# Queries and keys stored as rows 2d + s, in a LayerNorm + attention + mixture-of-experts kernel

## The chip, the cores and the metric

The kernel runs on one core of a Trainium2 chip. The metric is the device time of one execution in microseconds, as the median over several runs. Engines are called PE (TensorE), DVE (VectorE), ACT (ScalarE), POOL (GpSimd) and SP (SyncE, here only a queue that issues DMAs).

## What is computed

The input x has shape [2, 1024, 256]. It is normalized, and the output is x plus attention plus a mixture of experts, both of the normalized rows:

```python
xn = _layernorm(x, axis=-1)
x = x + attention(xn, W_q, W_k, W_v, W_o) + experts(xn, Wr, Wg, Wu, Wd)
```

Attention has 16 query heads of 16 dimensions and 4 heads of keys and values, each serving 4 query heads. Queries and keys are turned by rotary position angles, then softmax(q k / 4) v, then W_o. The experts: 8 of them, each token takes its top 2 by router logits, with a softmax gate over the two; an expert is silu(x Wg), clipped, times x Wu, times Wd. All of it is float32.

## The kernel before, in words

**Stages.** There are 2048 tokens, in 16 tiles of 128. First come LayerNorm, transposes, values and router logits, routing, and the projection of queries and keys (`queries_keys`). Then an expert loop over SLOTS = 39 slots, t = 0 to 38; a slot is one tile of 128 gathered token rows of one expert. Then attention over 8 head groups g (batch times key head), each in two halves h of 512 queries, so 16 halves.

**A slot of the expert loop.** POOL gathers the rows of slot t from xn_d in DRAM with an indirect DMA (`gather_rows`, L541, four row buffers go round; it waits until the transposes of slot t - 4 are done). PE does the gate and up product of slot t (`gate_up`, L1210), the transposes of slot t - 1's activations (L1218) and of slot t + 1's rows (L1203), and the down product of slot t - 2 (L1227). ACT does SiLU (L699) and copies the transposes (L702, L706), and stores finished rows to rows_out; DVE clips (L985), multiplies (L987) and copies the result (L993).

**Rope parts beside it.** The projected queries and keys are turned in 12 parts, at slots PART_SLOTS = 1, 3, 5, 7, 9, 11, 14, 17, 20, 23, 26, 29 (L307). In the order of PARTS (L302) parts 0, 1, 6 and 7 are keys (64 rows of 512 columns, made into 128 rows by two differences of column blocks), the others queries (128 rows of 512 columns). For part q, POOL or DVE multiplies by cos and sin (`times_cos`, `times_sin`, `rope_step`), DVE adds (L880, and L887, L889 for keys), ACT rounds to a high part (`high_part`, L683), DVE subtracts to get the low part (L899), and SP stores both to DRAM (`store_part`, L380). Buffers rope_a, rope_b, rope_hi and rope_low come four times (NB = 4), so `high_part(q)` waits until the stores of part q - 4 have landed (L682, through `stored_before`), and so does L899 (L898). ACT runs `high_part(5)` behind its work of slot 9.

**Rows.** A head's 16 dimensions are stored twice, as s = 0 (high) and s = 1 (low): q_hl has 32 rows for a head. Before, row s * 16 + d. The score product contracts 64 rows, in which high and low queries meet high (j = 0) and low (j = 1) keys.

**SP's queue** is in one order: all stores and loads that follow wait for what stands ahead of them. In the loop over the slots (L439) it stores part q at its slot; at t = 13 it waits for parts 0 and 1 to land (`parts_stored(1)`) and loads the key stack of group 0 (`load_ka`, 8 DMAs of 64 KB); at t = 14 it stores part 6 (keys), waits for parts up to 3 (`parts_stored(3)`) and loads the first queries (`load_q(0, 0, 0)`, L402, 4 DMAs of 128 KB); at t = 17 it stores part 7; at t = 18 it loads the second queries. Later slots load the second key stack (`load_kb`) and those of group 1 (LATE_LOADS).

**Scores beside the last slots.** From slot 18 = SLOTS - SHARED on, PE does the first scores of attention beside the slots (`first_max`, L1182, and `score_first`, L1149). The first of them, ahead of slot 18's gate product, waits for the first queries (`pe.wait_ge(q_loaded[v], 64)`, L1186).

**Attention.** ACT's exponentials (L740), PE's scores (L1280, L1284), products with values (L1294) and the score bounds of the half after next (L1155 to L1172), DVE's maxima (L934 to L942). In `period` SP loads kb of the next group, ka of the one after it and queries, a group ahead.

**Shapes of the accesses before.** A query store writes `[8, 16, 512]` from 128 partitions; a key store writes `[2, 64, 512]` from 128 partitions; a query load reads `[32, 2, 512]`; a load of ka or kb reads `[2, 16, 512]` (or fewer columns), its first dimension being a repetition of the same 16 rows, into 32 partitions.

Of the kernel before, what the change touches and what calls it, by code (L numbers as in the profile page):

```python
# [8 lines left out]
F32 = mybir.dt.float32  # L9
# [9 lines left out]
HD = 16  # L19
# [16 lines left out]
def build(nc, x, w_q, w_k, w_v, w_o, w_r, w_g, w_u, w_d, cos_t, sin_t, out):  # L36
# [3 lines left out]
    KV = w_k.shape[1] // HD  # L40
# [5 lines left out]
    HALF = S // 2  # L46
# [5 lines left out]
    NB = 4  # L52
# [14 lines left out]
    q_hl = nc.dram_tensor("q_hl", [B, NH, 2 * HD, S], F32, kind="Internal").ap()  # L67
    k_hl = nc.dram_tensor("k_hl", [B, 2, 2, KV * HD, 2 * HALF], F32, kind="Internal").ap()
# [3 lines left out]
    with ExitStack() as ctx:  # L72
        def sb(name, shape, dt=F32):
            return ctx.enter_context(nc.sbuf_tensor(name, shape, dt))
# [25 lines left out]
        rope_hi = [sb(f"rope_hi{m}", [P, HALF], F32R) for m in range(NB)]  # L100
        rope_low = sb("rope_low", [P, NB, HALF], F32R)
        rope_lo = [rope_low[:, m, :] for m in range(NB)]
# [199 lines left out]
        PARTS = [(k, m) for b in range(B) for k, m in ((2 * b, 2), (2 * b + 1, 2), (2 * b, 0), (2 * b, 1), (2 * b + 1, 0), (2 * b + 1, 1))]  # L302
# [19 lines left out]

        def stored_before(q):

            return 32 * len(range(q % NB, q, NB))


        def part_at(t):

            return PART_SLOTS.index(t) if t in PART_SLOTS else None  # L330
# [33 lines left out]
        def _(sp):  # L364
# [15 lines left out]
            def store_part(q):  # L380
                k, m = PARTS[q]
                n, done = q % NB, qk_stored[q % NB]
                b, cols = k // 2, slice(k % 2 * HALF, (k % 2 + 1) * HALF)
                sp.wait_ge(lo_ready, q + 1)
                if m < 2:
                    q_rows = q_hl[b, 8 * m:8 * m + 8, :, cols].rearrange("n (s d) q -> s n d q", s=2)
                    sp.dma_start(q_rows[0], rope_hi[n][:, 0:HALF].bitcast(F32)).then_inc(done, 16)
                    sp.dma_start(q_rows[1], rope_lo[n][:, 0:HALF].bitcast(F32)).then_inc(done, 16)
                else:
                    k_rows = [k_hl[b, k % 2, j].rearrange("d (u c) -> u d c", u=2) for j in range(2)]  # L390
                    sp.dma_start(k_rows[0], rope_hi[n][:, :].bitcast(F32)).then_inc(done, 16)
                    sp.dma_start(k_rows[1], rope_lo[n].bitcast(F32)).then_inc(done, 16)


            def load_q(g, h, i, heads=(0, 1)):
# [9 lines left out]
            def twice(g, j, half, cols):  # L405

                kv = g % KV
                return k_hl[g // KV, half, j, HD * kv:HD * (kv + 1), cols].unsqueeze(0).to_broadcast(
                    [2, HD, cols.stop - cols.start])

            def load_ka(g, p):

                for half in range(2):
                    for j in range(2):
                        low, high = 2 * HD * j, STACK + 2 * HD * j
                        sp.dma_start(ka[p][low:low + 2 * HD, half, :].bitcast(F32),
                                     twice(g, j, half, slice(QUART, KCOLS))).then_inc(ka_loaded[p], 16)
                        sp.dma_start(ka[p][high:high + 2 * HD, half, :].bitcast(F32),
                                     twice(g, j, half, slice(0, HALF))).then_inc(ka_loaded[p], 16)

            def load_kb(g, p):
                for half in range(2):
                    for j in range(4):
                        sp.dma_start(kb[p][2 * HD * j:2 * HD * (j + 1), half, :].bitcast(F32),
                                     twice(g, j % 2, half, slice(HALF - P, 2 * HALF - P))).then_inc(kb_loaded[p], 16)
# [9 lines left out]
            def parts_stored(last):  # L435
                for q in range(max(0, last - NB + 1), last + 1):
                    sp.wait_ge(qk_stored[q % NB], stored_before(q + NB))

            for t in range(SLOTS):  # L439
                q = part_at(t)  # L440
                if q is not None:
                    store_part(q)
                if t == KEYS_LOAD:
                    parts_stored(1)
                    load_ka(0, 0)
                if t == FIRST_LOAD:
                    parts_stored(3)
                    load_q(0, 0, 0)
                if t == SECOND_LOAD:
                    parts_stored(5)  # L450
                    load_q(0, 1, 1)
                for n in LATE_LOADS.get(t, ()):
                    sp.wait_ge(rows_t_ready, t)
                    if n == 0:
                        load_kb(0, 0)
                    elif n == 1:
                        load_ka(1, 1)
                    else:
                        load_q(1, (n - 2) // 2, 2 + (n - 2) // 2, [n % 2])
                if t == SLOTS - 7:  # L460
                    sp.wait_ge(m_turned_ready, 1)
                    load_m(0)
# [170 lines left out]
        def _(act):  # L633
# [44 lines left out]
            def high_part(q):  # L678
                n = q % NB
                act.wait_ge(rope_done, q + 1)  # L680
                if q >= NB:
                    act.wait_ge(qk_stored[n], stored_before(q))  # L682
                act.activation(rope_hi[n][:, :], rope_a[n][:, :], ACT.Copy).then_inc(hi_ready, 1)  # L683
# [67 lines left out]
        def _(dve):  # L751
# [140 lines left out]
            def rope_step(q):  # L892
                if 2 <= q <= NP + 1:
                    n = (q - 2) % NB
                    dve.wait_ge(hi_ready, q - 1)
                    dve.wait_ge(rope_done, q - 1)
                    if q >= NB + 2:
                        dve.wait_ge(qk_stored[n], stored_before(q - 2))  # L898
                    nc.vector.tensor_tensor(rope_lo[n], rope_a[n][:, :],  # L899
                                            rope_hi[n][:, :].bitcast(F32), ALU.subtract).then_inc(lo_ready, 1)  # L900
                if q < NP:
                    (k, m), n, rows_q = PARTS[q], q % NB, part_rows(q)
                    dve.wait_ge(pj_copied, 3 * k + m + 1)
                    if q >= NB:
                        dve.wait_ge(rope_done, q - NB + 1)
                    nc.vector.stream_shuffle(rope_b[n][0:rows_q, :], projected(k, m)[0:rows_q, :],
                                             [d ^ 1 for d in range(32)]).then_inc(swapped, 1)
                    if vector_cos(q):
                        if q >= NB:
                            dve.wait_ge(hi_ready, q - NB + 1)  # L910
                            dve.wait_ge(lo_ready, q - NB + 1)
                        nc.vector.tensor_tensor(rope_a[n][0:rows_q, 0:HALF], projected(k, m)[0:rows_q, :],
                                                cos_s[0:rows_q, k % 2 * HALF:(k % 2 + 1) * HALF], ALU.mult).then_inc(cos_done, 1)
# [507 lines left out]
```

## Time and profile before

| | us |
|---|---|
| median of 3 runs | 556.92 (556.55 to 557.96) |
| profiled execution, its time | 555.41 |
| its span | 553.6 |
| PE busy | 519.5 (94%) |
| DVE busy | 384.6 (69%) |
| ACT busy | 384.2 (69%) |
| POOL busy | 170.0 (31%) |
| mean granted clock of PE | 0.984 |

DMA moves 52.72 MB in 39266 packets, a mean of 95 GB/s. The chain of work that ended last is 79% PE, 8% DVE and 7% DMA, with 4% of the span under the stores of rope_low to k_hl and 2% under the loads of qs from q_hl.

The trace gives starts and durations in microseconds from the start of the span. Idle time stands in brackets with what released the engine. An issue on SP is timed as long as SP is held by it, which is not the time that the transfer takes; from issue to landing is given apart. A DMA share of 1/16 = 0.0625 is one of the 16 DMA engines busy. The granted clock is 1.00 at 2.4 GHz and 0.50 at 1.2 GHz.

### The profile page before, as it was taken

What the parts mean: (1) busy time and instruction counts of PE and PEld (TensorE: products, weight loads), DVE (VectorE), ACT (ScalarE), POOL (GpSimd) and SP (SyncE); (2) the same over time, 40 slices, a digit from 0 to 9 for tenths busy, and PEclk for the clock granted to TensorE, in tenths of its full rate; (3) what the DMA queues carried; (4) which work ended last, traced back from release to release, by engine and by line L of the source; (5) the groups of instructions that cost most, each with busy time, mean ns of one, the idle gap of its engine ahead of it and who ended that gap; (6) DMA issues with size and microseconds to landing.
All of it is one profiled execution on the core that took longest, in us unless ns stands there. A gap on an engine that the chain in (4) does not pass through costs nothing.

```text
span 553.6 us, 10341 instructions
## 1 busy us (share of the span) xinstructions
PE 519.5 (94%) x3626; PEld 247.9 (45%) x3626; DVE 384.6 (69%) x907; ACT 384.2 (69%) x551; POOL 170.0 (31%) x214
## 2 busy tenths in 40 slices
PE   8999987909999998999999999999999999999997
PEld 7833644504555554344444444444434444444433
DVE  4684886514787665778788788788787788885123
ACT  3534533302444335999999999999999999998673
POOL 4016654512232200032337332453245242510000
PEclk9999999958999999999999999999999999999999
DMA  8971455423345511131132131231132132200101
GB/s 292 374 219 38 113 153 161 147 93 113 119 140 164 153 38 40 41 95 41 60 96 67 53 96 49 68 96 52 55 92 76 48 92 59 58 3 22 49 28 58
DMA packets 39266, 52.72 MB, mean 95 GB/s; under 512 B 7632, under 2 KB 25424, under 8 KB 39216
## 3 DMA queue, kind: packets, MB, share of 16 engines
q1 hardware_dynamic: 26992, 34.35, 19.9%
q0 software_dynamic: 3408, 9.31, 6.0%
q10 hardware_dynamic: 8816, 8.40, 4.9%
q8 instruction: 30, 0.49, 0.4%
q14 instruction: 20, 0.16, 0.1%
HBM read 36.18 MB, written 15.60 MB: 94 GB/s over the span
## 4 chain that ended last, share of the span: by engine, by line
PE 79%; DVE 8%; DMA 7%; issue 3%; SPq 2%; ACT 1%; DVEq 0%; ACTq 0%
PE bank L1294 23%; PE bank L1284 10%; PE bank L1210 9%; PE bank L1155 9%; PE bank L1172 8%; PE bank L1227 4%; DMA k_hl<-rope_low 4%; PE bank L1124 4%; PE bank L1330 3%; PE bank L1280 3%; PE bank L1165 2%; DVE xn_t L942 2%; DVE xn L1019 2%; DMA qs<-q_hl 2%; PE bank L1114 1%
## 5 line engine op out<-in xcount | busy, mean ns | idle before, releaser
L740 ACT ACTIVATE big<-bank 128x1024 f32<-128x1024 f32 x256 | 249.7, 1024 | 11.8 <-PE bank L1284 11.1
L1294 PE MATMUL bank<-big,v_st 128*32 128x128 f32 (+2 forms) x1696 | 154.3, 436 | 2.8 <-DVE xn L1019 2.8
L1284 PE MATMUL bank<-qs,kb 64*128 64x512 f32 x512 | 130.4, 418 | 0.7 <-ACT big L740 0.7
L934 DVE TENSOR_REDUCE mx<-bank 128x1 f32<-128x512 f32 x128 | 87.8, 686 | 52.5 <-PE bank L1157 52.3
L688 ACT ACTIVATE xn_t<-bank 128x512 f32<-128x512 f32 x128 | 76.5, 598 | 35.7 <-PE bank L1157 27.5
L939 DVE TENSOR_REDUCE mx<-bank 128x1 f32<-128x512 f32 x128 | 87.4, 683 | 13.8 <-PE bank L1165 7.4
L942 DVE CUSTOM_DVE_ANT_0 xn_t<-bank,xn_t 128x512 f32<-128x512 f32 x128 | 87.8, 686 | 1.1
L1210 PE MATMUL bank<-big,xn 128*128 x156 | 77.7, 622 | 3.7 <-ACT xn L702 3.2
L1155 PE MATMUL bank<-ka,qs 64*128 64x512 f32 x128 | 63.6, 497 | 16.4 <-DMA qs<-q_hl 15.6
L1284 PEld LDWEIGHTS bank<-qs,kb 64*128 64x128 f32 x512 | 62.9, 185 | 28.4 <-ACT big L740 19.2
L1155 PEld LDWEIGHTS bank<-ka,qs 64*128 64x128 f32 x128 | 23.5, 184 | 96.4 <-DVE mx L939 58.0
L1157 PE MATMUL bank<-ka,qs 64*128 64x512 f32 x128 | 63.8, 499 | 0.0
L1172 PE MATMUL bank<-ka,qs 64*128 64x512 f32 x128 | 61.3, 479 | 0.0
L1294 PEld LDWEIGHTS bank<-big,v_st 128*32 128x32 f32 x1696 | 33.8, 108 | 56.9 <-issue 54.6
L618 POOL TENSOR_TENSOR xn<-xn,rden 128x256 f32<-128x256 f32 x15 | 9.5, 633 | 151.5 <-DVE rden L1023 141.1
L541 POOL DMA_INDIRECT xn<-xn_d,token_of x39 | 38.1, 977 | 57.4 <-PE bank L1203 46.1
L1165 PE MATMUL bank<-ka,qs 64*128 64x512 f32 x128 | 55.1, 430 | 0.0
L699 ACT ACTIVATE xn<-bank 128x256 f32<-128x256 f32 x39 | 14.9, 381 | 54.5 <-PE bank L1210 54.5
L985 DVE TENSOR_SCALAR xn<-xn 128x256 f32<-128x256 f32 x39 | 18.1, 465 | 43.2 <-ACT xn L699 43.2
L603 POOL TENSOR_SCALAR rope_a<-rope_a,gate 128x256 f32<-128x256 f32 x32 | 29.3, 921 | 54.0 <-DMA rope_a<-rows_out,place_i 54.0
L1227 PE MATMUL bank<-big,xn 128*128 x156 | 41.4, 389 | 1.6 <-DVE xn L993 1.6
L1210 PEld LDWEIGHTS bank<-big,xn 128*128 128x128 f32 x156 | 27.6, 193 | 31.9 <-issue 30.9
(147 smaller groups left out, 591.9 us busy)
## 6 DMA issues: line engine op xcount, KB each, us to landing
qs<-q_hl SPq DMA_DIRECT2D x64, 128.0 KB, 3.3
rows_out<-xn ACTq DMA_DIRECT2D x37, 128.0 KB, 5.2
ka<-k_hl SPq DMA_DIRECT2D x64, 64.0 KB
kb<-k_hl SPq DMA_DIRECT2D x64, 64.0 KB
xs<-in_L_attn_x SPq DMA_DIRECT2D x4, 512.0 KB, 6.4
big<-in_L_ffn_Wg SPq DMA_DIRECT2D x16, 128.0 KB, 6.8
big<-in_L_ffn_Wu SPq DMA_DIRECT2D x16, 128.0 KB, 6.9
big<-in_L_ffn_Wd SPq DMA_DIRECT2D x16, 128.0 KB, 6.8
```

The lines of the kernel that those rows point to most:

```text
L688: act.activation(gain[k % 2], max_bank(v, 4 * k), ACT.Relu).then_inc(gain_ready, 1)
L740: act.activation(probs[kt % 2][:, 2 * j:2 * j + 2, :].rearrange("p r q -> p (r q)"), st_ps[j][:, :], ACT.Exp, scale=1.0 / math.sqrt(HD)).t ...
L934: nc.vector.reduce_max(mx[h][:, STEPS + k, 0:1], max_bank(v, i), axis=X_AXIS).then_inc(mx_taken, 1)
L939: nc.vector.reduce_max(mx[h][:, STEPS + k, 1:2], max_bank(v, i), axis=X_AXIS).then_inc(mx_taken, 1)
L942: nc.vector.tensor_tensor_reduce(larger, max_bank(v, i + 1), gain[k % 2], scale=1.0, scalar=-FAR, op0=ALU.add, op1=ALU.max, accum_out=mx[h ...
L1155: mm(low.rearrange("p (c n) -> p c n", c=2), qs[q][0:STACK, j, rows], ka[p][0:STACK, :, QUART:HALF], start=True, stop=True).then_inc(mx_sc ...
L1157: mm(high.rearrange("p (c n) -> p c n", c=2), qs[q][STACK:P, j, rows], ka[p][STACK:P, :, 0:QUART], start=True, stop=True).then_inc(mx_scor ...
L1165: mm(max_bank(v, i).rearrange("p (c n) -> p c n", c=2), qs[q][STACK:P, j, rows], ka[p][STACK:P, :, QUART:HALF], start=True, stop=True).the ...
L1172: mm(max_bank(v, i).rearrange("p (c n) -> p c n", c=2), qs[q][0:STACK, j, rows], ka[p][0:STACK, :, 0:QUART], start=True, stop=True).then_i ...
L1210: last = mm(gu_ps[i % 2][:, :], rows_t[i % 2][:, c, :], wgu[:, e, c, :], start=(c == 0), stop=(c == C - 1))
L1284: last = mm(out[i], kb[p][half[i], kt // QT, keys], qs[q][half[i], j, :], start=False, stop=True, skip_group_check=kt % QT > 0)
L1294: last = mm(o_ps[32 * r:32 * (r + 1), columns], v_st[p][:, key_block(kt), :], probs[kt % 2][:, r, columns], start=(kt == 0 and columns.sta ...
```

## The change

In DRAM the 32 rows of a query head are now numbered 2d + s instead of s * 16 + d. So a store of queries has 128 rows of equal distance in its first dimension. A store of a key part, formerly two DMAs of 256 KB (high and low), becomes four of 128 KB, each of 64 partitions, with 64 rows in its first dimension. Each load of ka or kb names every key row twice in a row (16 x 2) instead of the 16 rows twice over (2 x 16), which gives the rows of the stack the order 2d + s too. `stored_before` counts 64 instead of 32 for a key part's landings. Loads of queries keep their shape.

```diff
         def stored_before(q):
-            return 32 * len(range(q % NB, q, NB))
+            return sum(32 if PARTS[o][1] < 2 else 64 for o in range(q % NB, q, NB))
...
                 if m < 2:
-                    q_rows = q_hl[b, 8 * m:8 * m + 8, :, cols].rearrange("n (s d) q -> s n d q", s=2)
+                    q_rows = q_hl[b, 8 * m:8 * m + 8, :, cols].rearrange("n (d s) q -> s (n d) q", s=2)
                     sp.dma_start(q_rows[0], rope_hi[n][:, 0:HALF].bitcast(F32)).then_inc(done, 16)
                     sp.dma_start(q_rows[1], rope_lo[n][:, 0:HALF].bitcast(F32)).then_inc(done, 16)
                 else:
-                    k_rows = [k_hl[b, k % 2, j].rearrange("d (u c) -> u d c", u=2) for j in range(2)]
-                    sp.dma_start(k_rows[0], rope_hi[n][:, :].bitcast(F32)).then_inc(done, 16)
-                    sp.dma_start(k_rows[1], rope_lo[n].bitcast(F32)).then_inc(done, 16)
+                    for u in range(2):
+                        rows_u, cols_u = slice(KV * HD * u, KV * HD * (u + 1)), slice(HALF * u, HALF * (u + 1))
+                        sp.dma_start(k_hl[b, k % 2, 0, :, cols_u], rope_hi[n][rows_u, :].bitcast(F32)).then_inc(done, 16)
+                        sp.dma_start(k_hl[b, k % 2, 1, :, cols_u], rope_lo[n][rows_u, :].bitcast(F32)).then_inc(done, 16)
...
-                return k_hl[g // KV, half, j, HD * kv:HD * (kv + 1), cols].unsqueeze(0).to_broadcast(
-                    [2, HD, cols.stop - cols.start])
+                return k_hl[g // KV, half, j, HD * kv:HD * (kv + 1), cols].unsqueeze(1).to_broadcast(
+                    [HD, 2, cols.stop - cols.start])
```

## Rows read from the trace of the kernel before

**Rows 1.** Windows: length, PE, PEld, DVE, ACT, POOL busy, clock, DMA share, GB/s

```profile
80.00:87.00 7.00, 3.28 (x13) 1.58 (x12) 4.15 (x9) 1.44 (x4) 3.67 (x4) 1.00 0.62 186
110.00:126.00 16.00, 0.41 (x2) 0.31 (x2) 2.83 (x6) 0.63 (x1) 2.60 (x2) 0.59 0.28 94
...
116.00:118.00 2.00, 0.00 (x0) 0.00 (x0) 0.00 (x0) 0.00 (x0) 0.00 (x0) 0.50 0.88 261
119.00:123.00 4.00, 0.00 (x0) 0.00 (x0) 0.00 (x0) 0.00 (x0) 0.00 (x0) 0.50 0.13 51
...
126.00:128.00 2.00, 2.00 (x4) 0.84 (x3) 0.69 (x1) 0.60 (x1) 0.00 (x0) 0.50 0.29 109
140.00:213.00 73.00, 71.31 (x270) 37.94 (x268) 52.97 (x128) 28.08 (x70) 16.74 (x18) 1.00 0.39 116
213.00:505.00 292.00, 287.83 (x2594) 121.81 (x2594) 236.04 (x536) 278.16 (x340) 97.80 (x121) 1.00 0.22 63
```

**Rows 2.** Timeline of PE: start, us, line, count, idle before

```profile
83.22 1.03 PE L1227 MATMUL bank<-big,xn 128*128 x4
86.88 1.98 PE L1210 MATMUL bank<-big,xn 128*128 x4 [2.63 <-ACT xn L702]
...
102.50 0.44 PE L1203 MATMUL bank<-ident,xn 128*128 128x128 f32 x2 [0.26 <-DMA xn<-xn_d,token_of]
102.80 1.13 PE L1227 MATMUL bank<-big,xn 128*128 x4
103.77 1.89 PE L1210 MATMUL bank<-big,xn 128*128 x4
...
106.79 1.88 PE L1210 MATMUL bank<-big,xn 128*128 x4
...
125.59 0.76 PE L1155 MATMUL bank<-ka,qs 64*128 64x512 f32 x1 [15.61 <-DMA qs<-q_hl]
...
126.31 3.70 PE L1210 MATMUL bank<-big,xn 128*128 x4
```

**Rows 3.** Chain that ended last, 58 to 135 us: start, us, what

```profile
62.55 22.93 DMA k_hl<-rope_low
...
85.56 0.44 ACT rope_hi L683
...
103.63 6.63 SPq L392
110.44 5.15 SPq L402
...
115.64 0.43 SPq L402
...
116.58 8.88 DMA qs<-q_hl
```

**Rows 4.** Timeline of SP's queue: start, us that SP is held, line

```profile
83.10 0.57 SPq L387 DMA_DIRECT2D q_hl<-rope_hi  x1
...
99.92 1.96 SPq L418 DMA_DIRECT2D ka<-k_hl  x1
103.08 0.51 SPq L391 DMA_DIRECT2D k_hl<-rope_hi  x1
...
117.14 0.48 SPq L391 DMA_DIRECT2D k_hl<-rope_hi  x1
```

**Rows 5.** Waits over the whole span: total, times, longest us

```profile
PE bank L1155 <- DMA qs<-q_hl: 15.6, 1, 15.6
```

**Rows 6.** Timeline of DVE, slot 9's sum of part 4

```profile
81.79 0.68 DVE L880 TENSOR_TENSOR rope_a<-rope_a,rope_b 128x512 f32<-128x512 f32 x1
```

**Rows 7.** Query loads (L402), issue to landing: 178 to 184 us, then 260 to 300

```profile
DMA to landing us min/median/max: 4.2/4.8/5.3
...
DMA to landing us min/median/max: 2.3/3.0/11.0
```

**Rows 8.** Gathers of token rows (L541), issue to landing, whole span

```profile
DMA to landing us min/median/max: 2.7/5.7/7.7
```

## The prediction

> **What bounds the kernel now.** I read the page's slices first, then stretches (windows), then the chain of waits, then the queues one by one. The windows [rows 1] show TensorE as the bound nearly everywhere: 71.31 us busy of the 73 from 140 to 213 (expert slots with the maxima beside them), 287.83 of 292 from 213 to 505 (attention). Two stretches are different: 80 to 87 us, where it works 3.28 us of 7, and 110 to 126 us, where it works 0.41 us of 16. Both lie in the expert loop. TensorE's own timeline [rows 2] gives the stalls exactly: slot 11's gate product starts at 86.88 after 2.63 us idle, and the first score of slot 18 starts at 125.59 after 15.61 us idle, which the waits put down to a load of qs.
>
> The chain of waits [rows 3] says what is behind each. The first stall: a store of keys, issued at 62.55, is what the chain follows for 22.93 us; it ends at 85.48, and ScalarE's `high_part(5)` (L683) may then overwrite rope_hi. The second: the key store of part 6 holds SP for 6.63 us at L392, the first load of queries behind it holds SP for another 5.15 us, and the last of the four loads takes 8.88 us more to land.
>
> Why are these transfers slow? From 119 to 123 us [rows 1] there is almost nothing in flight but key stores (issued from 117.1 on [rows 4]), and the DMA share is a steady 0.13, which is 2 engines of 16, at 51 GB/s. The key store's access has 2 rows in its first dimension. From 116 to 118 us, when the query loads ran, whose access has 32 rows there, the share was 0.88 and the rate 261 GB/s. So a 512 KB key part takes about 512/51 = 10.3 us, and the two parts stored at 56 and 62 us need 20.6 us in a row, which is the first stall. The Trainium skill (DMA: Bandwidth & Descriptors, Why a DMA increments its semaphore by 16 and not by 1) states that a copy runs on the largest number up to 16 that divides the slowest dimensions of both sides; by that rule the 2 of before agrees with the 0.13, and it says 16 for the shapes after, which no row of before shows for stores of these tensors.
>
> **The change part by part.**
>
> Key stores, 4 parts. Two issues of 256 KB become four of 128 KB, each with 64 rows first. An unblocked store issue on SP takes 0.57 us, as at 83.10 [rows 4], plus 0.04 between issues, so 2 more cost 1.22 us of SP per key part, 4.9 us for four; SP is not the bound, and only part 6, directly ahead of the first query load, has this on a path. Transfer: from 10.3 us at 51 GB/s to about 2 us at the 261 GB/s of rows 1; between these, anything above some 40% of that rate serves for what follows.
>
> Query stores, 8 parts: 8 rows first become 128; no count changes. Their waiters (L682, L898, four parts later) do not appear in the waits of before, so the gain is 0, hidden behind the slots between.
>
> Key loads ka and kb, 8 and 8 issues per head group: first dimension 2 becomes 16, the bytes and counts stay. No wait of TensorE on them exists in the trace (the only DMA wait of TensorE over 0.3 us is the one on qs [rows 5]); cover in attention is a half of a group, 292/14 = 20.9 us. Gain 0; if that cover were short, TensorE would show DMA waits at L1284, and it shows none. They also hold SP: the last of the eight at slot 13 is issued from 99.92 to 101.88 [rows 4], ahead of part 6, but is over before that part is ready.
>
> Row order 2d + s on both sides of the product only reorders the contraction: same matmuls, same columns, 0.
>
> **First stall.** With part 1 landed long before, `high_part(5)` waits for the sum at L880 instead: 81.79 + 0.68 = 82.47 [rows 6], start 82.51 rather than 85.56. SiLU and the copies behind it take as long as now (from 85.56 to 86.88 at TensorE is 1.32 us), so the product's rows are ready for 83.83. But TensorE is still in L1227 until 84.25 (83.22 + 1.03); where nothing is waited for, the next product starts 0.16 us before that modelled end (102.80 + 1.13 against 103.77 [rows 2]), so at 84.09. Gain 86.88 - 84.09 = 2.79 us. Next late is TensorE itself.
>
> **Second stall.** Everything moves up by 2.79. Part 6's low half releases SP at 103.08 - 2.79 = 100.29 [rows 4]. Four stores: 4 x 0.61 = 2.44, to 102.73; the checks of `parts_stored(3)` take 0.18, as between the end of L392 (103.63 + 6.63) and 110.44 [rows 3]; loads then start at 102.91, 103.38, 103.85 and 104.32 (0.43 + 0.04 each, the unblocked issue at 115.64). The landing of the last is the unknown. Bounds: 3.0 us, the median in attention at 260 to 300 us; 8.88 us, the present one, with the jam [rows 3, 7]. The nearest rows are the four loads at 178 to 184 us, right behind query stores in the same loop: 4.2 to 5.3 us. Those stores ran on few engines, so I take their minimum, 4.2: landed at 108.52. TensorE wants them at 125.59 - 15.61 - 2.79 = 107.19. A wait of 1.33 us stays, on the same line, and 14.28 us are gained. Queued behind TensorE's wait are only its own slot and the gathers of later slots, which wait for its transposes.
>
> **The clock.** From 119 us at the latest to 128 us the granted clock was 0.50 (1.2 GHz), after TensorE had been idle from 110; slot 18's gate product took 3.70 us at that level against 1.88 for slot 17's [rows 1, 2]. The 2.63 us pause at 84 us left the clock at 1.00. A pause of 1.33 us should do so too: gain 3.70 - 1.88 = 1.82 us.
>
> Sum: 2.79 + 14.28 + 1.82 = 18.89 us. The profiled execution has a span of 553.6 and a time of 555.41, so it becomes 534.7 and 536.5. It lay 1.5 us under the median of 556.92; the forecast for the median is 556.92 - 18.9 = **538.0 us**.
>
> A rule that speaks against the split of the key stores: the Trainium skill (DMA: Bandwidth & Descriptors, Rules for kernel authors) says two transfers to disjoint partition halves serialize, both spraying over all engines, and advises one transfer of 128 partitions. Here "before" is no such transfer (0.13 of the engines), so the rule leaves only the added issues, which the sum has at 1.22 us ahead of the query loads; were part 6 sent in two issues instead, the sum would be 1.22 us better, 536.8.
>
> **The rivals.**
>
> A, forecast: both stalls go but for about 1 us. 0.77.
>
> B, the query loads are still late. Against it: they are jammed now by an engine pair that is free after. For it: SP's stores of part 6 go out directly ahead, now over all sixteen engines, where the query loads, the gathers and the rows_out stores go too, and part 6 is ready only 7 us before TensorE wants the queries. Landing as now, 8.88: at 113.2, a wait of 6.0 instead of 1.33, and the clock falls again (1.82). Gain 18.89 - 4.68 - 1.82 = 12.4, 544.5 us. 0.15.
>
> C, the change doesn't spread what it should (the descriptor generator splits by something else than the first dimension). Then 20.6 us for two key parts stay; time 557, at most 1.5 us off. For it speaks only that no spread key store was seen. 0.05.
>
> D, slower. Traffic that now sits on two engines moves onto those that bring the gathered token rows. A gather lands in 2.7 to 7.7 us, median 5.7 [rows 8]; four row buffers go round, so with about 1.3 us of GpSimd between, a slot cannot be shorter than (landing + 1.3)/4, 1.75 us now against slots of 3.02 (one gate product to the next, 103.77 to 106.79 [rows 2]) and 4.1 with scores (21 slots from 126.31 to 213). The place is L1203's wait. To give back 18.9 us and 1.7 more, landings must be above 15.2 us: (15.2 + 1.3)/4 = 4.13, 1.11 more on 18 slots (20 us), 0.03 on 21 (0.6). At 17 us a slot is 4.58: 28 us and 10 us, less 18.9, so 576 us. The bytes do not change, and 512 KB at 261 GB/s adds 2 us at most to a gather; 0.03.
>
> **How the numbers follow.** What a measurement of this kernel can tell from no change is about 0.3%, 1.7 us. The low end takes the 3.0 us landing (1.2 us better), the 0.26 us that L1203 waits for a gather at 102.5 [rows 2], and about 1 us for the spread of the runs: 535.5. The high end is B's 544.5. Outside lie C, D and the tails. Faster: A and B, with little of their mass lost: 0.92. Same: C, 0.05. Slower: D, 0.03.
>
> **What would show it.** Right: no idle before slot 11's gate product; the key stores at L391/L392's place at 0.57 us each with none held for 5 us; the DMA share in the stretch after part 7's store well above 0.13; a wait of 0 to 2 us at L1155 in slot 18; the granted clock 1.00 throughout the loop; attention, 213 to 505 us, as long as before. B would show a wait over 3 us at L1155 and a clock of 0.50 behind it. C would show SP issues of 5 us at the stores. D would show waits of L1203 for gathers in most slots. What would make the sum wrong though its steps hold: a landing of the query loads outside 3 to 5 us, a wait of another engine uncovered once TensorE comes to slot 18 earlier (VectorE still has part 7 to turn there, L880 to L912), or attention changing its length.

## The result and the profile after

The change brings the median from 556.73 us (556.14 to 557.96, 4 runs) to 535.29 us (535.19 to 535.38, 4 runs): a ratio of 0.9612, 95% interval 0.9595 to 0.9629, 21.4 us less. The forecast was 538.0 us with a range from 535.5. So the direction and most of the size were right, and the time came out 0.2 us below the range. One run of the kernel before, beside e1 to e4, took 948.14 us at a granted clock of 1.00; it counts as a slow run and is in no ratio.

The windows of the kernel after, columns as in [rows 1]. They are the stretch in which the first stall lay, the slots around the new first score, and 292 us of attention (the last begins 19 us earlier than its counterpart, where the work has moved by 20.1, so its sums are not quite those of before):

```profile
80.00:87.00 7.00, 6.65 (x26) 3.89 (x25) 5.31 (x11) 2.50 (x7) 4.06 (x4) 1.00 0.47 151
...
103.00:110.00 7.00, 5.37 (x21) 2.82 (x20) 4.48 (x10) 2.32 (x6) 2.88 (x3) 1.00 0.73 197
...
194.00:486.00 292.00, 288.47 (x2596) 121.50 (x2595) 236.68 (x538) 278.70 (x340) 97.97 (x121) 1.00 0.22 63
```

TensorE works 6.65 us of the seven from 80 on, against 3.28 [rows 1]. There is no stretch of 16 us any more in which it does next to nothing, and the mean granted clock of the whole execution is 1.00. TensorE is as busy in attention as it was. TensorE's timeline, to be set beside [rows 2] (lines are one higher after the change):

```profile
79.24 1.88 PE L1211 MATMUL bank<-big,xn 128*128 x4
80.96 0.38 PE L1219 MATMUL bank<-ident,xn 128*128 128x128 f32 x2
...
82.77 1.98 PE L1211 MATMUL bank<-big,xn 128*128 x4 [0.35 <-ACT xn L703]
...
102.69 1.88 PE L1211 MATMUL bank<-big,xn 128*128 x4
...
107.50 0.47 PE L1156 MATMUL bank<-ka,qs 64*128 64x512 f32 x1 [1.63 <-DMA qs<-q_hl]
...
107.92 1.98 PE L1211 MATMUL bank<-big,xn 128*128 x4
...
111.56 1.98 PE L1211 MATMUL bank<-big,xn 128*128 x4
```

Slot 11's gate product starts at 82.77 instead of 86.88, the first score at 107.50 instead of 125.59, and slot 18's gate product takes 1.98 us instead of 3.70. Slot 19's starts at 111.56; before the change it started at 131.67 (the line below). Either kernel has 421.9 us of its span left from there (553.6 - 131.67, 533.5 - 111.56), so the whole gain has been made by then:

```profile
131.67 1.99 PE L1210 MATMUL bank<-big,xn 128*128 x4
```

The chain that ended last, from part 6 to the first score (start, us, what), for [rows 3]:

```profile
98.25 0.70 DVE rope_low L900
98.97 0.48 SPq L392
99.49 0.60 SPq L393
100.13 0.60 SPq L392
100.77 0.60 SPq L393
101.37 0.05 issue
101.55 0.46 SPq L403
...
102.99 4.37 DMA qs<-q_hl
```

In this stretch no issue holds SP for more than 0.60 us, where it was 6.63 and 5.15. The key stores of the first parts, which had kept ScalarE waiting until 85.5, no longer appear in the chain, and gathers and stores of rows are quicker too, though nothing was changed in them: a gather lands in a median of 3.6 us instead of 5.7 [rows 8],

```profile
DMA to landing us min/median/max: 2.8/3.6/4.4
```

and the stores of rows_out in 1.8 us instead of 5.2, by the pages' DMA issues.

### The profile page after: what moved, and what is told of

It is laid out like the page before. It is cut to its first block, busy times and chain, and to the rows that moved or that the text cites. A ratio compares the mean times of both kernels' runs of the same rounds, so it can differ in the third digit from the quotient of the medians.

```text
span 533.5 us, 10349 instructions
## 1 busy us (share of the span) xinstructions
PE 516.6 (97%) x3626; PEld 246.3 (46%) x3626; DVE 383.6 (72%) x907; ACT 384.3 (72%) x551; POOL 170.2 (32%) x214
## 4 chain that ended last, share of the span: by engine, by line
PE 85%; DVE 8%; issue 3%; ACT 2%; DMA 2%; SPq 1%; DVEq 0%; ACTq 0%
PE bank L1295 24%; PE bank L1211 11%; PE bank L1285 10%; PE bank L1156 9%; PE bank L1173 8%; PE bank L1228 5%; PE bank L1125 4%; PE bank L1331 3%; PE bank L1281 3%; PE bank L1166 2%; DVE xn_t L943 2%; DVE xn L1020 2%; PE bank L1115 1%; PE bank L1219 1%; PE bank L1204 1%
## 5 line engine op out<-in xcount | busy, mean ns | idle before, releaser
L741 ACT ACTIVATE big<-bank 128x1024 f32<-128x1024 f32 x256 | 249.7, 1024 | 11.9 <-PE bank L1285 11.1
L1211 PE MATMUL bank<-big,xn 128*128 x156 | 76.1, 610 | 1.8 <-ACT xn L703 1.2
L986 DVE TENSOR_SCALAR xn<-xn 128x256 f32<-128x256 f32 x39 | 16.4, 421 | 37.1 <-ACT xn L700 37.1
L1228 PE MATMUL bank<-big,xn 128*128 x156 | 41.3, 388 | 1.6 <-DVE xn L994 1.6
```

The lines of the kernel that those rows point to most:

```text
L741: act.activation(probs[kt % 2][:, 2 * j:2 * j + 2, :].rearrange("p r q -> p (r q)"), st_ps[j][:, :], ACT.Exp, scale=1.0 / math.sqrt(HD)).t ...
L1211: last = mm(gu_ps[i % 2][:, :], rows_t[i % 2][:, c, :], wgu[:, e, c, :], start=(c == 0), stop=(c == C - 1))
L1228: last = mm(y_ps[i % 2] if y is None else y, act_t[i % 2][:, c, :], wdn[:, e, c, :], start=(c == 0), stop=(c == C - 1))
```

## The experiments

They were run on three chips, each beside runs of the kernel before. On the first chip (e1 to e4) the kernel before took 556.58 us, on the second (e5 to e8) and third (e9 to e11) 565.65 and 566.55. The time is lost behind the expert loop: the last product of the loop in the change starts at 193.31 us in the first trace and at 193.34 in that of the third chip (e11), and 340.2 and 346.9 us of the span are left from there. So ratios are compared between chips, and of the traces only the part up to slot 19.

**The key stores alone.** Only the four DMAs of 64 rows (and the count of their landings), the rest as before:

```diff
-                    k_rows = [k_hl[b, k % 2, j].rearrange("d (u c) -> u d c", u=2) for j in range(2)]
-                    sp.dma_start(k_rows[0], rope_hi[n][:, :].bitcast(F32)).then_inc(done, 16)
-                    sp.dma_start(k_rows[1], rope_lo[n].bitcast(F32)).then_inc(done, 16)
+                    for u in range(2):
+                        rows_u, cols_u = slice(KV * HD * u, KV * HD * (u + 1)), slice(HALF * u, HALF * (u + 1))
+                        sp.dma_start(k_hl[b, k % 2, 0, :, cols_u], rope_hi[n][rows_u, :].bitcast(F32)).then_inc(done, 16)
+                        sp.dma_start(k_hl[b, k % 2, 1, :, cols_u], rope_lo[n][rows_u, :].bitcast(F32)).then_inc(done, 16)
```

> Only the key stores of the change (four DMAs of 64 rows for a part), rows still s * 16 + d, so query stores keep 8 rows first and the loads of ka and kb keep 2. Theory (the two-engine key stores make both stalls): both stalls go, 535.3 to 537.5 us; what it may miss against the change is a later landing of the first queries, since the eight two-row loads of ka at slot 13 still hold SP and two engines until about 100 us. Rival (the two-row loads are as much to blame for the second stall): a wait of 5 us or more stays at the first score of slot 18, 541 us or more.

Measured: 544.35 us, ratio 0.9788 (0.976 to 0.9816). Its timeline of TensorE:

```profile
82.74 1.98 PE L1211 MATMUL bank<-big,xn 128*128 x4 [0.34 <-ACT xn L703]
...
112.87 0.76 PE L1156 MATMUL bank<-ka,qs 64*128 64x512 f32 x1 [7.03 <-DMA qs<-q_hl]
113.59 3.78 PE L1211 MATMUL bank<-big,xn 128*128 x4
```

The first stall is gone as in the full change. Of the second 7.03 us stay, and with them the half clock (3.78 us for the gate product). My theory fell here and the rival held. What differs from the full change is the loads of ka and the stores of queries; the padded run below (e8), which has query stores of 8 rows too but the new loads (and the new numbering), waits only 1.73 us. So the loads of ka, which I had priced at nothing, hold up the queries by the other 5.3 us. They have as many issues and bytes in either form: only the order of the dimensions differs.

**All but the key stores.** The change, with the key stores and the count of their landings turned back.

> Everything of the change except the key stores, which go back to two DMAs with 2 rows first. Theory: the two key parts still need 20 us on two engines, both stalls stay (2 to 3 us before slot 11's gate product, 13 us or more at slot 18's first score, granted clock 0.50 behind it): 553 to 557 us. Rival (loads and query stores carry a good part of the gain): under 550 us.

Measured: 551.38 us, ratio 0.9908 (0.9881 to 0.9934).

```profile
86.37 3.52 PE L1210 MATMUL bank<-big,xn 128*128 x4 [3.98 <-ACT xn L702]
...
121.19 0.76 PE L1155 MATMUL bank<-ka,qs 64*128 64x512 f32 x1 [10.17 <-DMA qs<-q_hl]
```

Both stalls stay, the second at 10.17 us instead of 15.61 (13 or more was expected); the time lies between the two expectations. Alone, the key stores are worth 12.2 us and the rest 5.2 (of 556.58), together 21.2 (535.43, e3 below), which is 3.7 us more than their sum: both kinds of transfers stand ahead of the same query loads.

**Queues turned round in e1.** With e1's stores, the queries loaded at slot 13 ahead of the key loads:

```diff
                 if t == KEYS_LOAD:
-                    parts_stored(1)
-                    load_ka(0, 0)
-                if t == FIRST_LOAD:
                     parts_stored(3)
                     load_q(0, 0, 0)
+                    load_ka(0, 0)
```

> The key stores spread, all else as before (544.35 us, of which 7.03 us wait for the first queries), but with the first queries loaded at slot 13 ahead of the two-row key loads. If those 7 us come from the 512 KB of key loads that two engines work off ahead of the queries (10 us at 51 GB/s from 90 us on), the wait goes or moves to ka, whose loads then end at about 107 us, just when wanted: 535 to 537 us. Rival (two-row or eight-row transfers slow the query loads wherever they stand, or part 6's stores do): still over 541 us.

Measured: ratio 0.9732 (0.9674 to 0.9791). TensorE's first score:

```profile
111.01 0.76 PE L1154 MATMUL bank<-ka,qs 64*128 64x512 f32 x1 [5.13 <-DMA ka<-k_hl]
```

The wait has moved from the queries to ka, as expected, but is only 1.9 us shorter: ka landed at 110.8, not at 107. On the first chip's 556.58 us the ratio would be 541.7 us, so the time is the rival's (over 541) and the place of the wait is the theory's: neither expectation held whole.

**Before, with part 6 behind the queries.**

```diff
+                if t == FIRST_LOAD:
+                    parts_stored(3)
+                    load_q(0, 0, 0)
                 if q is not None:
                     store_part(q)
                 if t == KEYS_LOAD:
                     parts_stored(1)
                     load_ka(0, 0)
-                if t == FIRST_LOAD:
-                    parts_stored(3)
-                    load_q(0, 0, 0)
```

> The kernel before with nothing but SP's slot 14 turned round: the first queries are loaded ahead of key part 6. Theory (part 6's two-engine store holds SP 6.6 us and the engines 10 us ahead of the queries, so it carries most of the second stall): the queries, issued from about 102 us, land at 108 to 113 us instead of 125.5, the first stall stays: ratio to before 0.975 to 0.985. Rival (the pile-up ahead of part 6, from the two-row key loads, is what holds the queries): they land at 117 us or later, ratio over 0.988.

Measured: ratio 0.9828 (0.9807 to 0.9848), inside the expected ratios; the queries come at 115.1, 2 us later than expected:

```profile
86.53 1.98 PE L1210 MATMUL bank<-big,xn 128*128 x4 [3.31 <-ACT xn L702]
...
115.23 0.76 PE L1155 MATMUL bank<-ka,qs 64*128 64x512 f32 x1 [5.59 <-DMA qs<-q_hl]
```

So an order of two lines gives nearly half of what the change gives; but the first stall, in which no order is at fault, stays at 3.31 us.

**One estimate for all of them.** In the kernel before, parts 0 and 1, 1024 KB on two engines, were under way from 56.25 (SP's first issue of them) to 85.48 [rows 3], 29.2 us. That is 36 GB/s beside the loop's own traffic, not the 51 GB/s of the empty stretch [rows 1]. Count what these two engines have to move from the store of part 5 to the landing that slot 18 waits for. I assume that they carry all of a transfer with 2 rows first, a quarter of one with 8 (2 engines of 8), an eighth of one with 16 or more (2 of 16); only the share for 2 rows is measured.

| kernel | part 5, KB | ka | part 6 | queries | sum | from, us | + sum / 36 GB/s | landed, us |
|---|---|---|---|---|---|---|---|---|
| before | 128 | 512 | 512 | 64 | 1216 | 92.75 | 127.3 | 125.5 |
| e1 | 128 | 512 | 64 | 64 | 768 | 88.6 | 110.4 | 112.7 |
| e6 (waits for ka) | 128 | 512 | behind | 64 | 704 | 88.7 | 108.7 | 110.8 |
| e9 | 128 | 512 | behind | 64 | 704 | 92.4 | 112.4 | 115.1 |
| e2 (pause before part 6, so from there) | | | 512 | 64 | 576 | 104.1 | 120.5 | 121.1 |

Landings are those that end TensorE's waits. The estimate is within 2.7 us in all five, but it was made after them. It fits the reading that a transfer of 2 rows costs those behind it eight times what a spread one does, a store or a load alike. It holds only while the two engines are what the queries wait for: for the change it would give 102.6 us (part 6 and the queries, 128 KB, from 98.97), but the last query load was only issued at 102.99 and landed at 107.36.

**Query stores of 8 rows.** The first try changed nothing:

```diff
-                    q_rows = q_hl[b, 8 * m:8 * m + 8, :, cols].rearrange("n (d s) q -> s (n d) q", s=2)
+                    q_rows = q_hl[b, 8 * m:8 * m + 8, :, cols].rearrange("n (d s) q -> s n d q", s=2)
```

> The change, with the query stores back at 8 rows in the first dimension (same bytes, same rows 2d + s). In the trace of before, TensorE's load of the expert number from SBUF took 2.18 and 2.80 us in slots 8 and 10, against 0.3 to 1.1 in others, and cost 0.46 and 1.08 us of TensorE. Theory 1 (the pile-up behind the two-engine key stores slows that load): none over 1.2 us here, time within 0.5 us of the change's 535.3. Theory 2 (the eight-engine query stores running at that time do it): loads of 2 us come back in slots 8 and 10, 536 to 537 us.

Measured: 535.43 us, ratio 0.9641 (0.9614 to 0.9667). But this is the change itself, not a test: with rows 2d + s the head and the row have one common step, and the two dimensions seem to have become one of 128 rows either way. SP's issues speak for it, the same 0.32 to 0.45 us as in the change, where stores of 8 rows took 0.57 [rows 4]:

```profile
74.88 0.32 SPq L387 DMA_DIRECT2D q_hl<-rope_hi  x1
75.25 0.44 SPq L388 DMA_DIRECT2D q_hl<-rope_low  x1
```

So it serves as a repeat of the change. The real test has one row of padding for each head (`[B, NH, 2 * HD + 1, S]`, and `0:2 * HD` in store and load):

> The change with query stores truly of 8 rows first (padded q_hl; without padding the rows merged and the stores were those of the change). With the key stores spread nothing piles up, so the expectation is no difference: 535.1 to 535.9 us, all reads of the expert number under 1.2 us, SP's store issues at 0.57 instead of 0.32 and 0.45 us. Rival: the eight busy engines delay the first queries, 536 us or more.

Measured on the second chip: ratio 0.9641 (0.9567 to 0.9715), which covers the change's 0.9612. Its first score starts at 107.74 after a wait of 1.73 us, against 107.50 and 1.63:

```profile
107.74 0.47 PE L1156 MATMUL bank<-ka,qs 64*128 64x512 f32 x1 [1.73 <-DMA qs<-q_hl]
```

One read of the expert number took 1.54 us, over the 1.2 expected, without a pause of TensorE. In the traces, query stores of 8 or 128 rows make no difference of more than 0.3 us there; the times, whose interval is 1.5% wide, can't tell the expectation from its rival. Two of the four runs had a mean clock of 0.997 and took 546.84 and 547.95 us, the two at 1.00 took 541.93 and 542.83.

**Reads of the expert number.** Ahead of each slot TensorE's queue reads one number from SBUF (`load_expert`, L1196). Before, 15 reads between 57 and 112 us took (ns: minimum, median, maximum)

```profile
L1196 PEldq TENSOR_LOAD <-slot_ei x15: 298/833/2796, 57.2 to 106.8; - x15
```

and the change's 17 took

```profile
L1197 PEldq TENSOR_LOAD <-slot_ei x17: 301/547/853, 57.1 to 111.1; - x17
```

The two long ones of before, 2.18 us in slot 8 and 2.80 in slot 10, stand in front of TensorE's two pauses marked "issue" in its trace:

```profile
75.40 0.41 PE L1218 MATMUL bank<-ident,xn 128*128 128x128 f32 x2 [0.46 <-issue]
...
82.75 0.41 PE L1218 MATMUL bank<-ident,xn 128*128 128x128 f32 x2 [1.08 <-issue]
```

Is it the place in SBUF? The kernel before, with the number read from partition 96:

```diff
-                pe.reg_load(expert_reg[i], slot_ei[0:1, bass.ds(t, 1)])
+                pe.reg_load(expert_reg[i], slot_ei[96:97, bass.ds(t, 1)])
```

> The kernel before, where TensorE reads the expert number from partition 96 of slot_ei instead of partition 0 (all partitions hold the same). Theory 1 (the read shares a path of the low partitions with the piled-up DMAs): the reads of 2.18 and 2.80 us in slots 8 and 10 fall under 0.6 us. Theory 2 (the path is common to all partitions, or the time is not the memory's): they stay at 2 us or more. The time stays at about 556 us either way, since the first stall ends with the landing at 85.5 us.

```profile
L1196 PEldq TENSOR_LOAD <-slot_ei x15: 298/544/2529, 57.1 to 108.0; - x15
```

The longest is 2.53 us, in slot 8, so another partition does not help. Slot 10's fell to 1.38, but that is no work of the partition: in e9, which reads partition 0, it took 0.49. One run of 569.94 us stands beside runs of before from 562.13 to 568.84, which is too few to say anything of the time. Which transfers make it? e1 (two-row stores gone, eight-row stores there) had a maximum of 1.53 us, e2 (the reverse) one of 1.09. With both kinds of stores as before and only the new loads:

> Rows 2d + s and the change's loads, with both kinds of stores as before: key stores with 2 rows first, and query stores with 8, which needs one row of padding for a head in q_hl so that the rows can't be merged. Against e2 (551.38 us) it differs in the query stores alone. Theory: the long reads of the expert number (2 us or more in slots 8 and 10) need both kinds piled up, so they are back here, and the time is 551.4 to 553 us. Rival: they came from the two-row loads or by chance, so no read is over 1.2 us.

```profile
L1196 PEldq TENSOR_LOAD <-slot_ei x15: 297/712/2234, 57.3 to 108.3; - x15
```

The reads of 2.17 and 2.23 us are back in slots 8 and 10, with pauses of 0.46 and 0.52 us. Behind the first stall the clock fell here, as the gate product of slot 11 shows:

```profile
86.66 3.14 PE L1210 MATMUL bank<-big,xn 128*128 x4 [2.81 <-ACT xn L702]
```

Its ratio is 0.9894 (0.9832 to 0.9956), not to be told from e2's 0.9908; of 556.58 us it would be 550.7, and its interval takes in the expected times. So reads of over 2 us came in all four traces with both kinds of narrow stores: before, e5, e7, and e9, with one of 2.20 us in slot 8 and a pause of 0.49 behind it:

```profile
L1196 PEldq TENSOR_LOAD <-slot_ei x15: 298/489/2197, 57.3 to 106.6; - x15
```

None of the traces that lack one kind has a read of over 2 us; the longest is 1.54 (e8). What makes the read wait stays open.

**The change with the queries first.** The edit of e9, made in the changed kernel.

> The change, with SP's slot 14 turned round: the first queries are loaded before key part 6 is stored, whose data is ready only at 99 us. If the wait of 1.63 us at slot 18's first score is there only because the queries stand behind part 6 on SP and on the engines, it goes: 533.7 us. Rival (TensorE then waits there for something else, say VectorE's work on part 7, or part 6's later landing delays a part): 534.5 to 535.3 us.

Measured: 533.67 us (533.51 to 533.83, 5 runs), ratio 0.9592 (0.9571 to 0.9613), beside e3's 535.43, the change's twin, on the same chip. The first score follows slot 17 without a wait:

```profile
104.83 1.03 PE L1228 MATMUL bank<-big,xn 128*128 x4
105.79 0.50 PE L1156 MATMUL bank<-ka,qs 64*128 64x512 f32 x1
```

Both were run again on a third chip.

> The change with the first queries ahead of part 6 once more, beside the change itself (next run) on one chip: no wait of TensorE for a DMA in the loop, 0.3% faster than the change, every run at a clock of 1.00.

> The change itself again. Its wait of 1.6 us at slot 18's first score is short enough that the clock mostly stays; in two of five runs of its twin the mean clock was 0.996 to 0.997 and the time 2 us longer. The same is expected here in some runs, at 537 us against 535.3.

Measured: 542.05 us (ratio 0.9583, 0.9565 to 0.9601) and 542.61 us (0.9587, 0.9569 to 0.9604). The wait of 1.54 us is in the one trace and not in the other, but 0.1% between the medians is within the intervals. So the wait is gone on both chips, and 1.8 us of time were gained on the first; on this one the gain is not shown. Nor did the clock fall in any of the five runs of the change here: what I expected from e3's two slower runs (below) did not come, though e8, with a wait of 1.73 us at the same place, had two such runs.

## Why the prediction came out as it did

Two terms were mis-sized, by 1.3 us each: the first stall, and the step from the profiled run to the median. With either one put right, the whole range would have lain 1.3 us lower and held the measured time.

**First stall, wrong in size.** The forecast had slot 11's gate product at 84.09, "Next late is TensorE itself", from TensorE's work as it stood in the trace of before. It started at 82.77. The pauses of 0.46 and 1.08 us behind the long register reads lay ahead of it, and I had counted them into TensorE's own pace. In the trace of the change both are gone, and only 0.35 us of waiting for ScalarE came in their place. Measured gain by slot 11: 4.11 us, 0.08 of it there already at slot 0, against 2.79. This is the term of the sum that was mis-sized, by 1.3 us, and none of the things listed under what would make the sum wrong was this one. The traces above show that such pauses come where both kinds of narrow stores pile up; how stores make a read wait they don't show.

**Second stall, right in size, its cause incomplete.** Its steps moved 1.32 us ahead with slot 11, and held (the last two rows are lengths, the others times in the trace):

| step | forecast | measured |
|---|---|---|
| part 6 releases SP, at | 100.29 | 98.97 |
| last query load issued, at | 104.32 | 102.99 |
| TensorE wants the queries, at | 107.19 | 105.87 |
| issue of the last load to its landing | 4.2 | 4.37 |
| wait that stays | 1.33 | 1.63 |

The gain is 13.98 us for the 14.28 of the forecast. But "Key loads ka and kb ... Gain 0" is true of attention alone. With the key stores spread, the ka load at slot 13 was worth 5.3 to 5.4 us of this stall (e1's 7.03 less e8's 1.73 or the change's 1.63) and the half clock with it. I looked for TensorE's waits on ka, found none, and took that for cover; what waited was the transfer queued behind it. The change spreads the loads too, so the sum came out all the same: that was luck, and for the key stores alone the same argument gave 535.3 to 537.5 us where 544.35 were measured. Likewise the two key parts' 20.6 us at 51 GB/s did not explain a landing 29.2 us after the first issue. The loop's own traffic on the same two engines would explain it; no run takes that traffic away.

**The clock, right in size.** Forecast 1.82 us. From slot 18's gate product to slot 19's it was 5.36 us and is 3.64, 1.72 less, and the first score in front gained 0.30 (0.72 to 0.42 until the gate product): 2.02 us. The argument for it, that a pause of 1.33 us leaves the clock because one of 2.63 did, was thinner than it looked: pauses of 2.81 us in e7 and 3.11 in e5 were followed by a granted clock of 0.50.

**Sum.** 0.08 + 4.03 + 13.98 + 2.02 = 20.1 us, which is the difference of the spans, against 18.9.

**From the profiled run to the median, wrong.** The profiled execution "lay 1.5 us under the median of 556.92", and the forecast took the 18.9 us of the trace off that median, as if the 1.5 us would stay. After the change the profiled execution (535.32) lies at the median (535.29). So 20.1 us of the trace became 21.4 in the medians, and the 1.3 us between are the second half of the miss. The offset seems to belong to the stall: in the first chip's runs of before, those at a mean clock of 0.985 took 554.91 and 555.13 us, those at 0.979 to 0.982 from 556.49 to 557.71, and the profiled one had 0.984. All four runs of the change had 1.00 and lie within 0.2 us. In e3, the change's twin, three runs at 1.00 took 535.11 to 535.43 and two at 0.996 and 0.997 took 537.22 and 537.54: the wait of 1.6 us that stays seems to let the clock fall now and then, for 2 us, and e8's runs divide in the same way. This is a correlation; no run sets the clock.

**The rivals.** B's mechanism was there in small (1.63 us for 1.33), its size was not: the last query load landed in 4.37 us, not 8.88. C fell: the key stores landed in about 2.4 us each. D fell: gathers became faster, not slower, most likely since they had shared the two piled-up engines. No run splits the key stores into four and leaves 2 rows first, so the four issues are parted from the shape only in the loads of ka, where the count stays. The split key stores cost SP 2.40 us for part 6, from 98.97 to 101.37, as forecast (2.44), and e4 takes them off the queries' way altogether.

## What to carry to other kernels

Look at the first dimension of both sides of every DMA, and at the DMA share while nothing else runs: 0.13 is two engines of sixteen. Such a transfer costs most to what is queued behind it on those engines and on the issuing queue, so look for its price in the landings of the wide transfers behind it, not in waits for the narrow one. When a stall goes away, short pauses in front of it and the spread of the runs may be its work too, and go with it.

## What the runs showed of the hardware

- At a DMA share of 0.13, two engines of 16, key stores moved at 51 GB/s with almost nothing else under way (119 to 123 us, before), and at about 36 GB/s beside the loop's traffic (1024 KB in 29.2 us). In the change, a key store of 128 KB landed in about 2.4 us.
- A read of one number from SBUF into a register of TensorE's queue took 0.3 us at the shortest, and in slots 8 and 10 up to 2.80 us (before) and 2.23 (e7) while stores of 2 and of 8 rows piled up; moving it to another partition left one of 2.53 us (e5).
- Two dimensions of a DMA's access with a common step behaved as one: the same text gave issues of 0.57 us with padding (8 rows, e8), and without it 0.32 and 0.45 us (e3), as with 128 rows in the change.
- How long TensorE paused did not alone decide whether its clock fell. Before slot 11's gate product, pauses of 3.98 us in e2 and 2.81 in e7 were followed by products of 3.52 and 3.14 us, but pauses of 3.31 us in e9 and 2.63 in the kernel before by products of 1.98.
